# POOL's transfers by index without waits between them, and the heads' fetches moved from SyncE's queue to ACT's

## The chip, the cores and the metric

One core of one Trainium2 chip runs the kernel as one program. The metric is device time in microseconds (us). The engines are PE (TensorE, matrix products), DVE (VectorE), ACT (ScalarE), POOL (GpSimd) and SP (SyncE, which here only issues DMA transfers). Each engine works through its own list of instructions in order; a semaphore wait in that list holds up everything behind it on that engine and nothing on the others.

## The reference

A "macaron" block on x of 16 sequences x 512 tokens x 256 features, in float32: a mixture-of-experts feed-forward, attention, and the same feed-forward again.

```python
x = x + 0.5 * ffn(layernorm(x))
x = x + attention(layernorm(x))          # 16 heads of 16, ALiBi bias, 8 heads causal and 8 anti-causal
x = x + 0.5 * ffn(layernorm(x))

# ffn: 2 shared experts (256 -> 128 -> 256) for every token, and 16 routed ones (256 -> 64 -> 256)
out = einsum('tnm,nmd->td', silu(gs) * us, wd_s)
weights, indices = top_k(softmax(flat @ router_w), 2)
out += einsum('tem,emd->td', silu(g) * u * comb, wd_r)   # only the 2 chosen experts of a token count

# attention
out = softmax(q k^T / 4 + bias) v ; return out @ Wf + bf
```

## The kernel before

The unit of work is a sequence b (512 tokens, NT = 4 tiles of 128 partitions). Layer l = 0 is the first feed-forward, l = 1 the second. The sequences of a layer are worked in groups: (0 to 5), (6 to 15) in layer 0, and (0 to 6), (7 to 12), (13 to 15) in layer 1.

Routing. For each sequence DVE finds the two experts of each token and `position`, the row that the token gets in a DRAM tensor `sorted_x` in which the tokens of an expert lie together. POOL then **scatters** the normalised tokens `xn` there: 8 indirect transfers for each sequence and layer (2 choices x 4 tiles), each of 128 rows of 1 KB. When the whole group is in, tiles of 256 sorted rows are fetched by SP's queue (`t_x`, with the expert's weights `t_w`), PE multiplies, and the results go to `sorted_y`. For each sequence POOL then **fetches** its rows back (`y_tok<-sorted_y`, again 8 indirect transfers), and DVE's `combine` (L1646) adds them, weighted, to `x_att` (l = 0) or `x_ffn` (l = 1). There is one buffer `y_tok`, so the 8 fetches of the next sequence start behind the `combine` of this one; only the last group has four more, in `q_stack` and `k_stack`.

Waits of POOL. The scatters of a sequence count on 2 or 3 semaphores in turn (`sent[i][n % d]`), the fetches likewise (`gathered[i][n % d]`), where `apart_out` and `apart_back` give d: 3 for scatters of layer 0's first group and for fetches of layer 1 from sequence 6 on, else 2. Transfer n waits until transfer n - d has landed, so at most d of a sequence are under way:

```python
if n >= apart_out(l, b):
    pool.wait_ge(*sent[buffer][n % apart_out(l, b)].at(l, b, n - apart_out(l, b)))
```

Other work stands between these transfers in POOL's list: the causal masks of the attention weights (L1797 on `p_buf`, which PE's value products L1202 need), the low halves of the shared experts' hidden values (L1770 on `hs_buf`, which PE's down products L991 to L993 need), `qk_part` (L1784), `rstd` (L1726), and `o_pack` times the reciprocal `den` (L1803).

Heads. Attention handles 4 heads (a g of 4) at a time. PE leaves 4 heads' outputs and softmax denominators in a PSUM bank, ACT copies it to `o_raw` (L1350) and issues its transfer to DRAM, `o_store` (L1353). When g = 2m and 2m + 1 are there, the piece `heads` (b, m) fetches them back rearranged: `o_pack` (256 KB) and `den` (256 KB, each denominator row repeated for the 16 rows of its head). DVE takes the reciprocal of `den` in four parts (L1676), POOL multiplies, and PE projects (L1215) once both m are done. Before the change SP issues these two transfers (L925, L928), behind waits for both `o_store` transfers, for the projection of sequence b - 1, and for the last use of `den`.

The shift. For each g, ACT also sends 8 KB of row maxima into `q_stack` (L1367), and PE's score products of that g (L1182) wait for it.

Order. A planner (`Plan.run`) simulates the five engines with a cost and a due time for each piece and writes each engine's list; the engines then follow the lists, whatever the real times are. A piece `part(at, engine, cost, piece, needs..., takes..., lag)` is due at `at`, takes `cost`, and its result counts as there after `lag`. The planner knows the limit of d too (`some`), with a landing 2.2 us after the issue.

Of the kernel before, what the change touches and what calls it, by code (L numbers as in the profile page):

```python
# [15 lines left out]
B, S, D = 16, 512, 256  # L16
# [118 lines left out]
def y_buffer(l, b):  # L135
    return (b - Y_EARLY) % 5 if l == 1 and b >= Y_EARLY else 0

# [134 lines left out]
def schedule():  # L272
# [186 lines left out]
    for b in range(B):  # L459
# [32 lines left out]
        for m in range(2):  # L492
            heads = "heads", b, m
            at = t + 8 * m + 4 + 9.6
            part(at, "SP", 1.0, heads, (("o put", b, 2 * m), "ACT"), (("o put", b, 2 * m + 1), "ACT"),
                 takes=[(f"o_pack{m}", ("o_pack", b, m), [(("project", b, 1), "PE")]),
                        ("den", ("den", b, m), [(heads, "POOL")])], lag=4.0)
            for i in range(NT):
                part(at + 0.5 + 0.2 * i, "DVE", 0.85, ("heads", b, m, i), (heads, "SP"))
# [55 lines left out]
def build(nc, book, plan, a, out):  # L555
    ctx = ExitStack()
    with ctx:
# [147 lines left out]

        sent = [[signal(f"sent{i}{n}", 16) for n in range(3)] for i in range(6)]
        filled, filled_act = signal("filled", 16), signal("filled_act", 16)
        gathered = [[signal(f"gathered{i}{n}", 16) for n in range(3)] for i in range(5)]

        def all_sent(l, b):  # L710

            i, d = norm_buffer("ffn", l, b), apart_out(l, b)
            return [sent[i][n % d].at(l, b, n) for n in range(2 * NT - d, 2 * NT)]

        def all_gathered(l, b):
            i, d = y_buffer(l, b), apart_back(l, b)
            return [gathered[i][n % d].at(l, b, n) for n in range(2 * NT - d, 2 * NT)]
# [95 lines left out]
        def _(sp):  # L813
# [16 lines left out]
            def do(name, *of):  # L830
# [19 lines left out]
                elif name == "stack rows":  # L850

                    for b in EARLY:
                        sp.wait_ge(*x_put[0, b].at(b))
                        for landed in all_sent(0, b):
                            sp.wait_ge(*landed)
# [11 lines left out]
                elif name == "tile x":  # L867
                    l, g, j = of
                    i = x_home(l, g, j)
                    if j == 0:  # L870
# [7 lines left out]
                        for b in sent_all(l, g):  # L878
                            for landed in all_sent(l, b):
                                sp.wait_ge(*landed)  # L880
# [37 lines left out]
                elif name == "heads":  # L918
                    b, m = of
                    for i in range(2):  # L920
                        sp.wait_ge(*o_put[i].at(b, 2 * m + i))
                    if b:
                        sp.wait_ge(*proj_full.at(b - 1, 1))
                    heads = o_store[b, 2 * m:2 * m + 2].rearrange("g (h r) s -> (g h) r s", r=VR)
                    sp.dma_start(o_pack[:, m, :], heads[:, 0:HD, :]).then_inc(*o_got[m].step(b, 0))  # L925
                    if before["den", b, m]:
                        sp.wait_ge(*o_ready.at(*before["den", b, m][1:]))
# [297 lines left out]
        def _(act):  # L1225
            def do(name, *of):
# [37 lines left out]
                elif name == "norm":  # L1264
# [3 lines left out]
                    if before["xn", kind, l, b]:  # L1268
# [3 lines left out]
                        if old_kind == "ffn":  # L1272

                            for landed in all_sent(old_l, old):
                                act.wait_ge(*landed)
# [593 lines left out]
```

## Time and profile before

| what | us |
|---|---|
| median of 3 runs | 2264.89 |
| lowest and highest | 2262.14, 2269.9 |
| the profiled execution's own time | 2255.13 |
| its span, first to last instruction | 2253.3 |
| PE busy | 1702.2 (76%) |
| DVE busy | 1474.2 (65%) |
| ACT busy | 1046.5 (46%) |
| POOL busy | 947.3 (42%) |

Busy time counts neither waits nor the issuing of transfers by SP and ACT. A POOL indirect transfer counts as busy while POOL writes its descriptors (about 1 us). "POOL y_tok L1763 <- DMA" in a view of waits is idle time of POOL ahead of line 1763 that the landing of a transfer ended. The chain that ended last is followed back from the last instruction, at each step to what released it.

### The profile page before, as it was taken

The numbers are of one execution on the slowest core, as the hardware profiler recorded it, in microseconds if no ns is written. First come the engines' busy times: TensorE is split into PE (matmuls) and PEld (weight loads), VectorE is DVE, ScalarE is ACT, GpSimd is POOL, SyncE is SP. The second block draws the span as 40 slices with busy tenths as digits, with TensorE's granted clock in tenths as the row PEclk, the third lists the DMA queues.
The fourth block names the chain that finished last, engine by engine and source line by source line (L and its number), as shares of the span: only waits on it lengthen the run. The fifth ranks groups of instructions, "written<-read, shape, count | busy, mean of one in ns | idle before, by whom it ended". The sixth has DMA issues, their size and how long they took to land.

```text
span 2253.3 us, 35352 instructions
## 1 busy us (share of the span) xinstructions
PE 1702.2 (76%) x10696; PEld 1121.1 (50%) x10696; DVE 1474.2 (65%) x3920; ACT 1046.5 (46%) x2263; POOL 947.3 (42%) x999
## 2 busy tenths in 40 slices
PE   3758875678788888886877889888887677985382
PEld 2646655446455555543544546555554334553251
DVE  4765666677766657676677776766787757573432
ACT  3325543354455555554454555645554335553151
POOL 2643337454423231445444343443545635234604
PEclk8979996789999999988998989999998789997686
DMA  7468753645867666555449765666746686864895
GB/s 206 139 205 248 251 182 97 121 90 154 227 180 211 187 193 172 151 96 124 92 75 239 182 171 146 178 167 138 176 105 132 207 247 164 244 188 149 265 310 162
DMA packets 327979, 392.80 MB, mean 174 GB/s; under 512 B 40296, under 2 KB 269032, under 8 KB 327784
## 3 DMA queue, kind: packets, MB, share of 16 engines
q1 hardware_dynamic: 269520, 284.59, 48.4%
q0 software_dynamic: 24576, 67.14, 10.5%
q10 hardware_dynamic: 33696, 38.81, 5.2%
q8 instruction: 88, 1.44, 0.3%
q14 instruction: 99, 0.81, 0.1%
HBM read 188.58 MB, written 155.19 MB: 153 GB/s over the span
## 4 chain that ended last, share of the span: by engine, by line
PE 29%; DMA 26%; DVE 17%; issue 10%; POOL 10%; SPq 4%; ACT 3%; another core or an unknown queue 0%; ACTq 0%; DVEq 0%; POOLq 0%
DMA sorted_x<-xn,position 7%; DMA y_tok<-sorted_y,position 6%; DMA den<-o_store 4%; PE bank L1202 3%; PE bank L1098 3%; PE bank L991 3%; PE bank L1109 3%; PE bank L993 3%; PE bank L992 3%; PE bank L1182 2%; POOL sorted_x L1737 2%; DMA q_stack<-shift_t 2%; DVE x_att L1646 2%; PE bank L1215 2%; POOL y_tok L1763 2%
## 5 line engine op out<-in xcount | busy, mean ns | idle before, releaser
L1343 ACT ACTIVATE p_buf<-bank 128x512 f32<-128x512 f32 x640 | 361.8, 599 | 264.4 <-PE bank L1182 212.1
L1574 DVE TENSOR_REDUCE row_max<-bank 128x1 f32<-128x512 f32 (+2 forms) x768 | 349.2, 504 | 76.4 <-PE bank L1165 70.6
L1737 POOL DMA_INDIRECT sorted_x<-xn,position x224 | 221.4, 988 | 232.6 <-DMA sorted_x<-xn,position 140.4
L1797 POOL TENSOR_SCALAR_AFFINE_SELECT p_buf<-p_buf 128x512 f32<-128x512 f32 x256 | 161.6, 645 | 316.5 <-ACT p_buf L1343 314.9
L1182 PE MATMUL bank<-q_stack,k_stack 101*128 101x512 bf16 (+3 forms) x1024 | 244.7, 318 | 57.2 <-DMA q_stack<-shift_t 46.6
L1149 PE MATMUL bank<-k_stack,q_stack 99*128 99x512 bf16 (+3 forms) x1024 | 254.2, 319 | 32.4 <-issue 19.6
L1763 POOL DMA_INDIRECT y_tok<-sorted_y,position x192 | 185.5, 966 | 213.2 <-DMA y_tok<-sorted_y,position 117.0
L1202 PE MATMUL bank<-p_buf,v_rows 128*32 128x512 f32 (+3 forms) x2048 | 197.5, 485 | 91.0 <-POOL p_buf L1797 88.0
L1309 ACT ACTIVATE t_y<-bank 128x256 f32<-128x256 f32 x406 | 133.3, 380 | 156.4 <-PE bank L1109 137.4
L991 PE MATMUL bank<-w_down,hs_buf 128*128 128x256 f32 x256 | 89.1, 348 | 126.5 <-POOL hs_buf L1770 125.4
L1676 DVE RECIPROCAL den<-den 128x128 f32<-128x128 f32 x128 | 110.0, 913 | 101.2 <-DMA den<-o_store 99.8
L1098 PE MATMUL bank<-t_xt,t_w 128*128 128x256 f32 x548 | 156.8, 413 | 21.2 <-DMA t_w<-expert_w 12.1
L1165 PE MATMUL bank<-cbf 128*128 128x256 bf16 (+1 forms) x640 | 169.7, 265 | 0.0
L1182 PEld LDWEIGHTS bank<-q_stack,k_stack 101*128 101x128 bf16 x1024 | 85.4, 101 | 162.3 <-issue 61.8
L1627 DVE SCALAR_TENSOR_TENSOR t_g<-t_th,bank 64x256 f32<-64x256 f32 x203 | 82.5, 406 | 119.3 <-ACT t_th L1300 110.2
L1149 PEld LDWEIGHTS bank<-k_stack,q_stack 99*128 99x128 bf16 x1024 | 94.2, 102 | 127.3 <-issue 67.1
L1294 ACT ACTIVATE t_xt<-bank 128x512 f32<-128x512 f32 x203 | 118.7, 596 | 64.3 <-PE bank L1088 50.6
L1300 ACT ACTIVATE t_th<-bank 64x256 f32<-64x256 f32 x203 | 76.3, 376 | 147.3 <-PE bank L1098 105.7
L1202 PEld LDWEIGHTS bank<-p_buf,v_rows 128*32 128x32 f32 x2048 | 50.0, 115 | 171.2 <-POOL p_buf L1797 112.4
L991 PEld LDWEIGHTS bank<-w_down,hs_buf 128*128 128x128 f32 x256 | 60.4, 236 | 140.5 <-issue 139.7
L1098 PEld LDWEIGHTS bank<-t_xt,t_w 128*128 128x128 f32 x548 | 102.0, 202 | 53.6 <-issue 24.3
L1632 DVE TENSOR_TENSOR t_h<-bank,t_g 64x128 f32<-64x128 f32 x406 | 119.2, 293 | 13.3
(193 smaller groups left out, 3910.7 us busy)
## 6 DMA issues: line engine op xcount, KB each, us to landing
t_w<-expert_w SPq DMA_DIRECT2D x137, 256.0 KB
t_x<-sorted_x SPq DMA_DIRECT2D x137, 256.0 KB
sorted_y<-t_y SPq DMA_DIRECT2D x137, 256.0 KB
q_stack<-qk_part SPq DMA_DIRECT2D x192, 128.0 KB
k_stack<-qk_part SPq DMA_DIRECT2D x192, 128.0 KB
sorted_x<-zeros SPq DMA_DIRECT2D x69, 256.0 KB, 3.6
p_buf<-expert_w SPq DMA_DIRECT2D x66, 256.0 KB
p_buf<-sorted_x SPq DMA_DIRECT2D x66, 256.0 KB
```

Source lines behind the costliest of these rows:

```text
L991: pe.matmul(dst, left(0), right(0), start=first, stop=False, skip_group_check=True)
L1098: ins = pe.matmul(ps[:, 0:RT], weights[:, P * d:P * d + P], xt[:, d, :], start=(d == 0), stop=(d == ND - 1))
L1149: pe.matmul(ps[:, col:col + k1 - k0], q_stack[0:ROWS_S, h, P * qt:P * qt + P], k_stack[0:ROWS_S, h, k0:k1], start=(n == 0), stop=False, sk ...
L1165: ins = pe.matmul(dst, ident_bf, mask, start=False, stop=True, skip_group_check=True)
L1182: ins = pe.matmul(ps[:, col:col + q1 - q0], k_stack[0:ROWS_P, h, P * kt:P * kt + P], q_stack[0:ROWS_P, h, q0:q1], start=(n == 0), stop=Tru ...
L1202: ins = pe.matmul(ps[VR * hh:VR * hh + VR, q0:q1], v_rows[b % 2][:, v0:v0 + VR], p_of(u)[:, col:col + q1 - q0], start=(r == 0), stop=(r == 2),
L1309: act.activation(t_y[i][:, t, :], psum("ty", *of, t)[:, 0:D], ACT.Copy).then_inc(*ty_out.step(*of, t))
L1343: act.activation(p_of(u), psum("score", *of)[:, :], ACT.Exp).then_inc(*exp_done.step(*of))
L1574: ins = dve.tensor_reduce(row_max[g % 2][:, n:n + 1], src[:, col:col + q1 - q0], X, ALU.max)
L1737: pool.indirect_dma_start(sorted_x[l, group_of(l, b)], bass.IndirectOffsetOnAxis(ap=position[:, b, k, t:t + 1], axis=0), xn[buffer][:, t, ...
L1763: pool.indirect_dma_start(y[:, k, t, :], None, sorted_y[l, g], bass.IndirectOffsetOnAxis(ap=position[:, b, k, t:t + 1], axis=0)).then_inc( ...
L1797: pool.affine_select(blocks, blocks, [[0, GH], [1 if ahead else -1, P]], ALU.is_ge, zero, base=0, channel_multiplier=-1 if ahead else 1).t ...
```

## The change

Two things. (1) POOL issues the 8 scatters and the 8 fetches of a sequence without waiting for landings between them; one semaphore for each buffer counts all 8, and whoever needs them waits for the full count. (2) The piece `heads` goes from SP's list to ACT's, with a planned cost of 1.2 instead of 1.0 us. The planner still plans with the limit d, but since the piece is on another engine, it writes other lists for all engines from sequence 0's first `heads` on.

```diff
@@ planner @@
-            part(at, "SP", 1.0, heads, (("o put", b, 2 * m), "ACT"), (("o put", b, 2 * m + 1), "ACT"),
+            part(at, "ACT", 1.2, heads, (("o put", b, 2 * m), "ACT"), (("o put", b, 2 * m + 1), "ACT"),
...
-                part(at + 0.5 + 0.2 * i, "DVE", 0.85, ("heads", b, m, i), (heads, "SP"))
+                part(at + 0.5 + 0.2 * i, "DVE", 0.85, ("heads", b, m, i), (heads, "ACT"))
@@ semaphores @@
-        sent = [[signal(f"sent{i}{n}", 16) for n in range(3)] for i in range(6)]
+        sent = [signal(f"sent{i}", 16) for i in range(6)]
-        gathered = [[signal(f"gathered{i}{n}", 16) for n in range(3)] for i in range(5)]
+        gathered = [signal(f"gathered{i}", 16) for i in range(5)]
...
-            i, d = norm_buffer("ffn", l, b), apart_out(l, b)
-            return [sent[i][n % d].at(l, b, n) for n in range(2 * NT - d, 2 * NT)]
+            return sent[norm_buffer("ffn", l, b)].at(l, b, 2 * NT - 1)
@@ SP, and now ACT @@
-                elif name == "heads":
-                    ... sp.wait_ge, sp.dma_start ...
+                elif name == "heads":
+                    b, m = of
+                    for i in range(2):
+                        act.wait_ge(*o_put[i].at(b, 2 * m + i))
+                    if b:
+                        act.wait_ge(*proj_full.at(b - 1, 1))
+                    heads = o_store[b, 2 * m:2 * m + 2].rearrange("g (h r) s -> (g h) r s", r=VR)
+                    act.dma_start(o_pack[:, m, :], heads[:, 0:HD, :]).then_inc(*o_got[m].step(b, 0))
+                    if before["den", b, m]:
+                        act.wait_ge(*o_ready.at(*before["den", b, m][1:]))
+                    act.dma_start(den[:, :], heads[:, HD:VW, :].broadcast_to((HB, HD, S))).then_inc(*o_got[m].step(b, 1))
@@ POOL, scatter @@
-                    if n >= apart_out(l, b):
-                        pool.wait_ge(*sent[buffer][n % apart_out(l, b)].at(l, b, n - apart_out(l, b)))
...
-                        xn[buffer][:, t, :], None).then_inc(*sent[buffer][n % apart_out(l, b)].step(*of))
+                        xn[buffer][:, t, :], None).then_inc(*sent[buffer].step(*of))
@@ POOL, fetch @@
-                    y, landed = tail_y[y_buffer(l, b)], gathered[y_buffer(l, b)][n % apart_back(l, b)]
-                    if n >= apart_back(l, b):
-                        pool.wait_ge(*landed.at(l, b, n - apart_back(l, b)))
+                    y, landed = tail_y[y_buffer(l, b)], gathered[y_buffer(l, b)]
```

POOL's list before at the scatters of layer 1, sequence 3 (927 us in the profile); `sent00` and `sent01` are the two landing counts.

```order
L1770 TENSOR_TENSOR hs_buf<-h_buf,hs_buf 128x512 [waits h_hi]
L1797 AFFINE_SELECT p_buf<-p_buf 128x4x128 [waits exp_done]
L1737 DMA sorted_x<-xn,position 86272x256 [waits place_step]
L1737 DMA sorted_x<-xn,position 86272x256
L1737 DMA sorted_x<-xn,position 86272x256 [waits sent00]
L1737 DMA sorted_x<-xn,position 86272x256 [waits sent01]
L1737 DMA sorted_x<-xn,position 86272x256 [waits sent00]
L1737 DMA sorted_x<-xn,position 86272x256 [waits sent01]
L1770 TENSOR_TENSOR hs_buf<-h_buf,hs_buf 128x512 [waits h_hi]
L1737 DMA sorted_x<-xn,position 86272x256 [waits sent00]
L1737 DMA sorted_x<-xn,position 86272x256 [waits sent01]
L1797 AFFINE_SELECT p_buf<-p_buf 128x4x128 [waits exp_done]
```

POOL's list now at the same scatters.

```order
L1755 TENSOR_TENSOR hs_buf<-h_buf,hs_buf 128x512 [waits h_hi]
L1725 DMA sorted_x<-xn,position 86272x256 [waits place_step]
L1725 DMA sorted_x<-xn,position 86272x256
L1782 AFFINE_SELECT p_buf<-p_buf 128x4x128 [waits exp_done]
L1755 TENSOR_TENSOR hs_buf<-h_buf,hs_buf 128x512 [waits h_hi]
L1725 DMA sorted_x<-xn,position 86272x256 x2
L1769 TENSOR_TENSOR qk_part<-rest,qk_part 128x512 [waits qk_second]
L1725 DMA sorted_x<-xn,position 86272x256 x2
L1782 AFFINE_SELECT p_buf<-p_buf 128x4x128 [waits exp_done]
L1782 AFFINE_SELECT p_buf<-p_buf 128x4x128
L1725 DMA sorted_x<-xn,position 86272x256 x2
L1788 TENSOR_TENSOR o_pack<-o_pack,den 128x512 [waits den_done,o_got0]
```

Only the first scatter still waits for something (the positions). A `qk_part` and two more masks now also stand among the scatters, and `o_pack` follows them at once.

SP's list before at `heads` (1, 1), 634 us in the profile.

```order
L939 DMA k_stack<-qk_part 16x8x512 [waits qk_third,score_full]
L939 DMA k_stack<-qk_part 16x8x512 x5
L901 DMA sorted_y<-t_y 128x2x256 [waits ty_out]
L925 DMA o_pack<-o_store 128x1x512 [waits proj_full,o_put1,o_put0]
L928 DMA den<-o_store 128x1x512 [waits o_ready]
L883 TENSOR_LOAD tile_i [waits tx_full]
L884 ISA
L884 DMA t_x<-sorted_x 128x2x256
```

ACT's list before from `o_raw` of sequence 1, g = 3 on (625 us in the profile).

```order
L1350 ACTIVATE o_raw<-bank 128x512 [waits o_put0,o_full]
L1353 DMA o_store<-o_raw 128x512 [waits o_copied]
L1309 ACTIVATE t_y<-bank 128x256 [waits ty_put_sp1,ty_full]
L1309 ACTIVATE t_y<-bank 128x256
L1294 ACTIVATE t_xt<-bank 128x512 [waits tgu_full,tx_full]
L1343 ACTIVATE p_buf<-bank 128x512 [waits score_full] x2
L1239 ACTIVATE act_t<-bank 128x512 [waits qk_full,v_full,xt_full]
L1343 ACTIVATE p_buf<-bank 128x512 [waits score_full]
L1239 ACTIVATE act_t<-bank 128x512 [waits xt_full]
L1300 ACTIVATE t_th<-bank 64x256 [waits th_step,tgu_full]
L1343 ACTIVATE p_buf<-bank 128x512 [waits o_full,score_full]
L1343 ACTIVATE p_buf<-bank 128x512 [waits score_full]
```

ACT's list now, from the same `o_raw` on.

```order
L1332 ACTIVATE o_raw<-bank 128x512 [waits o_put0,o_full]
L1335 DMA o_store<-o_raw 128x512 [waits o_copied]
L1291 ACTIVATE t_y<-bank 128x256 [waits ty_put_sp2,ty_full]
L1291 ACTIVATE t_y<-bank 128x256
L1325 ACTIVATE p_buf<-bank 128x512 [waits score_full]
L1276 ACTIVATE t_xt<-bank 128x512 [waits tgu_full,tx_full]
L1325 ACTIVATE p_buf<-bank 128x512 [waits score_full]
L1222 ACTIVATE act_t<-bank 128x512 [waits qk_full,v_full,xt_full]
L1282 ACTIVATE t_th<-bank 64x256 [waits th_step,tgu_full]
L1358 DMA o_pack<-o_store 128x1x512 [waits proj_full,o_put1,o_put0]
L1361 DMA den<-o_store 128x1x512 [waits o_ready]
L1282 ACTIVATE t_th<-bank 64x256 [waits th_step,tgu_full]
```

The two transfers stand seven pieces behind the `o_store` transfer (counting the two rows of `t_y` as one), and wait there for its landing and for the projection; they no longer stand behind SP's transfers into `k_stack`. Tile work and scores follow them in ACT's list.

## Rows read from the trace of the kernel before

**Rows 1.** The page, head and part 1: busy us (share) and instructions.
```profile
span 2253.3 us, 35352 instructions
...
PE 1702.2 (76%) x10696; PEld 1121.1 (50%) x10696; DVE 1474.2 (65%) x3920; ACT 1046.5 (46%) x2263; POOL 947.3 (42%) x999
```

**Rows 2.** The chain that ended last, whole span: shares by line; then start, us, what.
```profile
by line: issue 10.4%; DMA sorted_x<-xn,position 6.8%; DMA y_tok<-sorted_y,position 6.3%; DMA den<-o_store 3.5%; PE bank L1202 3.5%; PE bank L1098 3.5%; PE bank L991 3.0%; PE bank L1109 2.8%; PE bank L993 2.7%; PE bank L992 2.6%; PE bank L11
...
634.58 9.19 DMA den<-o_store
...
1637.37 4.59 DMA den<-o_store
```

**Rows 3.** Waits, whole span: us in total, times, longest us.
```profile
POOL sorted_x L1737 <- DMA sorted_x<-xn,position: 140.4, 80, 5.2
...
POOL y_tok L1763 <- DMA y_tok<-sorted_y,position: 117.0, 62, 5.6
...
DVE den L1676 <- DMA den<-o_store: 99.8, 23, 11.7
...
PE bank L1182 <- DMA q_stack<-shift_t: 46.6, 19, 7.6
```

**Rows 4.** Timeline of POOL, 925 to 947 us: start, us, idle before.
```profile
931.96 0.96 POOL L1737 DMA_INDIRECT sorted_x<-xn,position  x1 [2.62 <-DMA sorted_x<-xn,position]
...
938.43 0.96 POOL L1737 DMA_INDIRECT sorted_x<-xn,position  x1 [4.25 <-DMA sorted_x<-xn,position]
...
940.85 1.27 POOL L1770 TENSOR_TENSOR hs_buf<-h_buf,hs_buf 128x512 fp32r<-128x512 f32 x1
```

**Rows 5.** Timeline of PE, 934 to 944 us.
```profile
942.38 0.55 PE L991 MATMUL bank<-w_down,hs_buf 128*128 128x256 f32 x1 [6.05 <-POOL hs_buf L1770]
```

**Rows 6.** Timeline of POOL in the first group, 60 to 112 us.
```profile
81.89 1.03 POOL L1737 DMA_INDIRECT sorted_x<-k_stack,position  x1 [0.18 <-issue]
...
92.05 0.98 POOL L1737 DMA_INDIRECT sorted_x<-k_stack,position  x1 [0.30 <-issue]
```

**Rows 7.** Line 1763, all transfers whose landing is known.
```profile
DMA to landing us min/median/max: 2.7/2.9/4.1
```

**Rows 8.** Windows: us, busy us of each engine, clock, DMA share, GB/s.
```profile
165.00:420.00 255.00, 194.12 (x1057) 144.40 (x1056) 153.65 (x472) 109.03 (x257) 115.65 (x111) 0.88 0.65 192
420.00:1715.00 1295.00, 1064.90 (x7081) 675.70 (x7079) 916.99 (x2305) 675.63 (x1425) 532.88 (x574) 0.92 0.63 155
1715.00:1880.00 165.00, 113.15 (x664) 65.64 (x665) 110.48 (x274) 60.56 (x124) 84.19 (x93) 0.82 0.72 201
2000.00:2253.00 253.00, 134.22 (x745) 90.45 (x743) 108.26 (x307) 80.00 (x197) 102.16 (x106) 0.76 0.68 220
```

**Rows 9.** Waits of PE, 420 to 1715 us.
```profile
PE bank L1202 <- POOL p_buf L1797: 64.7, 40, 6.7
PE bank L991 <- POOL hs_buf L1770: 41.1, 10, 6.8
```

**Rows 10.** Waits of PE, 165 to 420 us.
```profile
PE bank L991 <- POOL hs_buf L1770: 24.7, 5, 15.3
```

**Rows 11.** Waits, 1715 to 1880 us.
```profile
POOL y_tok L1763 <- DMA y_tok<-sorted_y,position: 33.3, 17, 4.7
```

**Rows 12.** Waits of POOL, 2000 to 2253 us.
```profile
POOL sorted_x L1737 <- DMA sorted_x<-xn,position: 11.8, 8, 2.7
```

**Rows 13.** The chain, 600 to 650 us: start, us, what.
```profile
625.27 0.33 ACTq L1353
...
633.85 0.68 SPq L925
```

**Rows 14.** The page, part 3: DMA queues (q1 SP's, q0 POOL's, q10 ACT's).
```profile
q1 hardware_dynamic: 269520, 284.59, 48.4%
q0 software_dynamic: 24576, 67.14, 10.5%
q10 hardware_dynamic: 33696, 38.81, 5.2%
```

## What the change should do, before it was run

> **What bounds the kernel now.** I read the page first. PE is busy for 76% of the span, ACT for 46%, POOL for 42% [rows 1], so no engine is full and the time is set by how they wait for each other. The chain that ended last says where: the landings of indexed transfers are 6.8% + 6.3% of 2253.3 us, 153 + 142 = 295 us, and those of `den` 3.5%, 79 us [rows 2]. The reader is to see that no line of PE has more than 3.5%. The waits say who stood: POOL sat idle 140.4 us for landings of scatters and 117.0 us for landings of fetches, 257 us in 142 waits, 1.8 us each; DVE 99.8 us for `den` [rows 3].
>
> An idle POOL costs nothing by itself, so next comes what stood behind it in its list. In the timeline at 926 us POOL waited 2.62 and 4.25 us for scatters that nobody else needed yet, then ran the `hs_buf` subtraction at 940.85 [rows 4], and PE, idle for 6.05 us, started its down product behind that at 942.38 [rows 5]. 6.87 us of POOL's waiting thus became 6.05 us of PE's. Between 420 and 1715 us PE waited 64.7 us for masks and 41.1 us for `hs_buf`, both POOL's work [rows 9]; between 165 and 420 us it was 24.7 us [rows 10]. The windows give the room: PE idle for 61 of 255, 230 of 1295, 52 of 165 and 119 of 253 us [rows 8].
>
> **The change: waits of POOL.** What is left of a transfer is its issue, 0.96 to 1.0 us, and 0.30 us between two. The first group shows eight scatters and one subtraction going out with hardly a wait: from 81.89 to 92.05 us seven intervals, less 1.3 us for the subtraction, make (10.16 - 1.3) / 7 = 1.27 us each [rows 6]. Eight take 10.2 us. I take the gain stage by stage, each between nothing (all hidden behind another chain) and POOL's whole idle time.
> - 165 to 420 us: at most the 24.7 us of [rows 10]. The same stretch also waits for inputs to be loaded and stored; I take half, 12 us.
> - 420 to 1715 us: PE waited 64.7 + 41.1 = 105.8 us for POOL [rows 9]. A mask may be late because ACT's exponentials were, which the change leaves as they are; I take half, 53 us, between 0 and 105.8.
> - 1715 to 1880 us: fetches into the one `y_tok`, DVE's sum, the next fetches. Everything is in series, and POOL's landing waits of 33.3 us [rows 11] lie on it. The last landing of eight will come somewhat later than now against its issue; I take 28 us.
> - 2000 to 2253 us: POOL waited 11.8 us for scatters [rows 12] and a little for fetches, with the transfer engines at 68% and 220 GB/s [rows 8], the highest rate of the four; 8 us.
>
> Together 101 us; bounds 0 and 257.
>
> How fast a landing is decides this. Where a landing of a fetch is known by itself it took 2.7 to 4.1 us, 2.9 in the middle [rows 7]; in the loaded stretch a pair held POOL for 4.25 us more after 0.30 us and an issue of 0.96 us each [rows 4]. The Trainium skill, "DMA: Bandwidth & Descriptors", section on the anatomy of one DMA on the gpsimd path, fits 2.0 us plus bytes over 436e3 to a transfer: 2.3 us for these 128 KB. By that estimate POOL would stand 1.0 us instead of 0.30 behind a pair, three times in each of 64 sets of eight: 134 us in all, and the term would be half of mine, about 50 us. The trace has 257 us of idle time, and I go by it.
>
> **The change: heads on ACT.** Removed from SP: 32 times two issues. At 625.27 us ACT sent off `o_store`; SP issued `o_pack` at 633.85 for 0.68 us [rows 13], behind stack transfers in its list, and `den`, issued at 634.58, took 9.19 us to land; another one took 4.59 [rows 2]. SP's queue carried 284.59 MB and was busy 48.4% of the span, ACT's 38.81 MB and 5.2% [rows 14], so on ACT's queue `den` has less ahead of it. 79 us on the chain at 9.19 us are about 9 landings. Halfway to 4.59 us saves 2.3 us each, 21 us (bounds 0 and 41).
>
> Added to ACT: two issues of about 0.68 us [rows 13], 1.4 us, 32 times, 44 us. ACT is busy 46% [rows 1]; scores for PE stand behind them, and a quarter on the path makes 10 us (bounds 0 and 44). ACT also waits there for the landing of `o_store`. Six pieces lie between, and SP, whose list has the same wait, was through it 8.6 us after `o_store` was sent off [rows 13]; I cost this wait at nothing, covered by those six pieces. Without them ACT would stand for up to 8.6 us each time. Last, the 8 KB shift of the next g follows 512 KB of heads on ACT's queue. PE already waits 46.6 us for shifts, 19 times of 64 [rows 3]. If half of the 19 come 1 us later, that is 10 us (bounds 0 and 64).
>
> **Contention.** No byte is added, but bursts are denser: up to eight of POOL's transfers under way for two or three now. 67.14 MB in 24576 packets is 2.7 KB a packet, SP's 1.06 KB [rows 14], so where both queues are full POOL's takes the larger share. Others then wait: 5 us, between 0 and the rival's price below. The other lists of the planner I cost at nothing either way: same pieces, other neighbours; random shifts of some us.
>
> **Sum.** 2255 (the profiled execution's own time) - 101 - 21 + 10 + 10 + 5 = 2158. The median of the runs shown is 2264.9, 9.8 us above that execution, so I add 10 for the usual run: 2168 us, 4.3% faster. Its own range is 2080 to 2235.
>
> **Rivals.**
> 1. Another chain is as long. POOL comes free, but PE at 82% in the long stretch (1065 of 1295 us, [rows 8]), DVE and the loads take over after a third of the gain: 34 us, about 2232. For it: only PE's 6.05 us of idle time, in one place, is shown to follow from POOL's waits. Against it: PE has 230 us idle there.
> 2. All of POOL's idle time comes back, with a shorter chain for everyone: 2265 - 257 = 2008. It needs every wait on the path; most of the 142 waits aren't.
> 3. The waits move into the issue: with more than three or four transfers under way the descriptor queue is full and POOL stands in its issue instead. Then only a few us change, 2265. For it: the trace never has eight of a sequence in flight under load. Against it: the issues of [rows 6] take 1.0 us each for a whole sequence and more.
> 4. Slower: POOL's bursts and the heads push back the 8 KB shifts and `den`. Each of 64 shifts has PE's scores of four heads behind it. At 2 us more each that is 128 us, less the 101 + 21 above: about 2271, and from 1.9 us a shift on the change loses. For it: packets of POOL's queue are 2.6 times as large as SP's [rows 14]. The Trainium skill, "DMA: Bandwidth & Descriptors", section on queues, rings and completion order, says that each DMA engine takes turns between its queues packet by packet, which by itself speaks for a larger share of large packets. Against it: the shift is a transfer of ACT's queue and gets its turn early, and the transfer engines were busy only 63% [rows 8].
>
> **Chances.** Forecast (2% to 8% faster) 0.60; rival 1 (0.3% to 2%) 0.14; rival 2 0.04; rival 3 0.07; rival 4 0.15. A measurement here can tell about 0.3% from no change. Faster 0.60 + 0.14 + 0.04 = 0.78, same 0.07, slower 0.15. The range of 8 in 10 reaches from 2080 to 2266: rival 1 and half of rival 3 are inside, rival 2 and rival 4 out.
>
> **What would show it.** POOL's idle time for landings ahead of its scatters and fetches is gone, and issues follow each other at 1.27 us with no issue above 1.7 us (rival 3: issues of several us). PE's waits for masks and `hs_buf` fall from 105.8 to about 50 us in the long stretch; the windows of the single `y_tok` shorten by 4 us a sequence. `den` lands in 6 to 7 us, and DVE's wait for it falls below 80 us. PE's wait for shifts stays under 60 us; above 100 us rival 4 holds. ACT's wait for `o_store` is under 20 us in all. The prediction is wrong if PE's idle time is merely booked to other releasers, or if ACT stands in `heads` for landings or for the projection of sequence b - 1, which I couldn't price from a row.

## The result

The changed kernel takes 2194.3 us (median of 4 runs, 2189.3 to 2198.2) against 2263.5 us before (4 runs). The ratio is 0.969 [0.966, 0.9721]: 3.1% faster. The forecast was 2168 us, 4.3% faster, with a range of 2080 to 2266 us.

The page of the changed kernel, head and parts 1 and 3 (queues: packets, MB, share):

```profile
span 2196.4 us, 35275 instructions
...
PE 1697.9 (77%) x10696; PEld 1117.4 (51%) x10696; DVE 1469.6 (67%) x3920; ACT 1043.5 (48%) x2263; POOL 949.1 (43%) x999
...
q1 hardware_dynamic: 260816, 267.81, 47.0%
q0 software_dynamic: 24576, 67.14, 10.9%
q10 hardware_dynamic: 42400, 55.59, 8.1%
```

Against [rows 1] no engine has less to do; the span is 57 us shorter and the shares went up by one or two points. Against [rows 14] the heads' 16.8 MB went from q1 to q10.

Its waits over the whole span (us in total, times, longest us; L1725 is the scatter, L1748 the fetch, L1667 the reciprocal, L1165 the score product, L974 the down product):

```profile
DVE den L1667 <- DMA den<-o_store: 102.0, 26, 11.8
...
POOL sorted_x L1725 <- issue: 61.4, 225, 0.5
...
PE bank L1165 <- DMA q_stack<-shift_t: 45.3, 16, 5.3
...
POOL y_tok L1748 <- issue: 42.1, 152, 2.2
...
PE bank L974 <- POOL hs_buf L1755: 38.6, 8, 15.0
```

Of [rows 3] both POOL rows are gone: no transfer by index waits for a landing any more, only for the 0.3 us of issue between two. DVE's wait for `den` did not fall (99.8, now 102.0 us), and PE's for the shift neither rose nor fell by much (46.6, now 45.3). The value product's group on the page shows PE's idle time for masks:

```profile
L1185 PE MATMUL bank<-p_buf,v_rows 128*32 128x512 f32 (+3 forms) x2048 | 188.8, 467 | 26.6 <-POOL p_buf L1782 19.2
```

That is 19.2 us where it was 88.0; PE's wait for `hs_buf` went from 125.4 to 38.6. But one wait of the same kind, the longest, has only changed its name in the view. Before, in layer 1's last sequence, it is put down to POOL:

```profile
2124.98 0.55 PE L991 MATMUL bank<-w_down,hs_buf 128*128 128x256 f32 x1 [29.80 <-POOL hs_buf L1770]
```

In the changed kernel the profile names no releaser, yet POOL's subtraction ends at 2067.43 us and PE starts at 2067.69:

```profile
2066.15 1.28 POOL L1755 TENSOR_TENSOR hs_buf<-h_buf,hs_buf 128x512 fp32r<-128x512 f32 x1
2067.69 0.55 PE L974 MATMUL bank<-w_down,hs_buf 128*128 128x256 f32 x1 [26.13 <-issue]
```

Counted with POOL's, PE's waits for masks and `hs_buf` go from 213.4 to 84 us. PE thus waits some 130 us less for POOL, and the span is 57 us shorter. Where the other 73 us went is the question of this study.

The same place as in [rows 4] and [rows 5], scatters of layer 1, sequence 3, in POOL's timeline now (start, us, idle before):

```profile
903.22 0.96 POOL L1725 DMA_INDIRECT sorted_x<-xn,position  x1 [0.30 <-issue]
904.49 0.96 POOL L1725 DMA_INDIRECT sorted_x<-xn,position  x1 [0.30 <-issue]
905.76 0.96 POOL L1725 DMA_INDIRECT sorted_x<-xn,position  x1 [0.31 <-issue]
907.03 0.96 POOL L1725 DMA_INDIRECT sorted_x<-xn,position  x1 [0.30 <-issue]
910.74 1.27 POOL L1755 TENSOR_TENSOR hs_buf<-h_buf,hs_buf 128x512 fp32r<-128x512 f32 x1 [2.75 <-ACT hs_buf L1246]
```

The first six scatters start at 900.59 us, 901.96 and from there on every 1.27 us, and at the second `hs_buf` subtraction POOL now waits for ACT (2.75 us), where before ACT had been ready and POOL stood for landings. The work behind the transfers is as early as ACT lets it be. By the two timelines POOL's list is the same at this place before and after: six scatters, the subtraction, two scatters, a mask. The list that is given above under "POOL's list now at the same scatters" is the one at the scatters of sequence 4 (987 us in the changed kernel), so that the `qk_part` and the masks between the scatters are no news of sequence 3.

**Where the time came from.** The lists are marked by the start of the reciprocals of sequence 0's first heads, of sequence 12's second, and of sequence 14's first. Before, these marks lie at 481, 1713 and 1895 us (windows: us, busy us of PE, PEld, DVE, ACT, POOL, clock, DMA share, GB/s):

```profile
0.00:481.00 481.00, 330.58 (x1849) 248.03 (x1850) 299.81 (x935) 193.93 (x426) 222.06 (x220) 0.87 0.61 177
481.00:1713.00 1232.00, 1018.81 (x6781) 648.68 (x6780) 875.13 (x2203) 642.86 (x1362) 499.18 (x540) 0.93 0.63 158
1713.00:1895.00 182.00, 127.57 (x757) 74.83 (x753) 124.81 (x316) 72.14 (x148) 97.75 (x105) 0.84 0.70 196
1895.00:2253.00 358.00, 225.22 (x1313) 149.58 (x1313) 174.48 (x467) 137.57 (x330) 128.33 (x135) 0.81 0.72 216
```

In the changed kernel they lie at 466, 1681 and 1847 us:

```profile
0.00:466.00 466.00, 329.84 (x1832) 250.74 (x1832) 303.95 (x936) 192.14 (x424) 221.13 (x219) 0.87 0.62 183
466.00:1681.00 1215.00, 1017.36 (x6792) 641.47 (x6792) 867.86 (x2200) 642.37 (x1363) 506.42 (x546) 0.93 0.65 160
1681.00:1847.00 166.00, 129.05 (x790) 77.34 (x790) 125.46 (x334) 74.45 (x158) 93.75 (x100) 0.87 0.79 222
1847.00:2196.00 349.00, 221.68 (x1287) 147.81 (x1285) 172.32 (x453) 134.55 (x319) 127.80 (x134) 0.81 0.71 217
```

The reader is to see four differences: -15 us up to the first mark, -17 us in the long stretch, -16 us in the 182 us after it, -9 us at the end. In the long stretch PE's idle time went from 1232 - 1019 = 213 to 1215 - 1017 = 198 us. Its waits for POOL there had been, before,

```profile
PE bank L1202 <- POOL p_buf L1797: 61.1, 37, 6.7
...
PE bank L991 <- POOL hs_buf L1770: 35.1, 9, 6.8
```

96.2 us, and in the changed kernel (L1185 the value product, L974 the down product) they are

```profile
PE bank L1132 <- issue: 31.9, 10, 10.1
PE bank L1165 <- DMA q_stack<-shift_t: 31.1, 12, 5.0
PE bank L1092 <- DVE t_h L1624: 18.2, 11, 6.3
PE bank L1185 <- POOL p_buf L1782: 13.0, 20, 1.7
PE bank L1071 <- DMA t_x<-sorted_x: 10.5, 4, 7.7
...
PE bank L1154 <- DVE shift L1660: 9.8, 8, 2.0
...
PE bank L974 <- POOL hs_buf L1755: 3.8, 3, 1.8
```

13.0 + 3.8 = 16.8 us (L1185 and L974). So 79 us of waits for POOL went away and 15 us of idle time went with them; the rest came back ahead of the row products (L1132, 31.9 us for which the profile shows no releaser, 11.6 before), the tiles that SP loads (L1071, 10.5 for 3.8) and the shift's transpose (L1154, 9.8 for 4.0), and in many smaller pieces. With all rows of the view added up by who came last, PE's waits in this stretch went from 97 to 20 us for POOL, from 46 to 64 for DVE, from 4 to 18 for ACT, and from 16 to 43 where the profile shows no releaser.

### The profile page after: what moved, and what is told of

It reads as the page before. It is cut to its first block and busy times, and to the rows that moved or that the text cites. A ratio compares the mean times of both kernels' runs of the same rounds, so it can differ in the third digit from the quotient of the medians.

```text
span 2196.4 us, 35275 instructions
## 1 busy us (share of the span) xinstructions
PE 1697.9 (77%) x10696; PEld 1117.4 (51%) x10696; DVE 1469.6 (67%) x3920; ACT 1043.5 (48%) x2263; POOL 949.1 (43%) x999
## 5 line engine op out<-in xcount | busy, mean ns | idle before, releaser
L1132 PE MATMUL bank<-k_stack,q_stack 99*128 99x512 bf16 (+3 forms) x1024 | 254.3, 320 | 64.6 <-issue 44.3
L1165 PE MATMUL bank<-q_stack,k_stack 101*128 101x512 bf16 (+3 forms) x1024 | 244.6, 321 | 67.5 <-DMA q_stack<-shift_t 45.3
L1725 POOL DMA_INDIRECT sorted_x<-xn,position x224 | 221.8, 990 | 101.5 <-issue 52.9
L1748 POOL DMA_INDIRECT y_tok<-sorted_y,position x192 | 186.1, 969 | 118.9 <-issue 42.1
L1185 PE MATMUL bank<-p_buf,v_rows 128*32 128x512 f32 (+3 forms) x2048 | 188.8, 467 | 26.6 <-POOL p_buf L1782 19.2
L1667 DVE RECIPROCAL den<-den 128x128 f32<-128x128 f32 x128 | 110.2, 915 | 102.1 <-DMA den<-o_store 102.0
L1132 PEld LDWEIGHTS bank<-k_stack,q_stack 99*128 99x128 bf16 x1024 | 92.8, 102 | 166.2 <-issue 101.8
L1165 PEld LDWEIGHTS bank<-q_stack,k_stack 101*128 101x128 bf16 x1024 | 87.6, 102 | 164.7 <-issue 57.5
L974 PE MATMUL bank<-w_down,hs_buf 128*128 128x256 f32 x256 | 88.5, 346 | 68.8 <-POOL hs_buf L1755 38.6
L1092 PE MATMUL bank<-t_w,t_h 64*128 64x256 f32 x548 | 102.8, 453 | 32.6 <-DVE t_h L1624 27.3
L1755 POOL TENSOR_TENSOR hs_buf<-h_buf,hs_buf 128x512 fp32r<-128x512 f32 x64 | 81.7, 1277 | 100.4 <-ACT hs_buf L1246 98.1
```

Of the source, the lines that this page charges most:

```text
L1132: pe.matmul(ps[:, col:col + k1 - k0], q_stack[0:ROWS_S, h, P * qt:P * qt + P], k_stack[0:ROWS_S, h, k0:k1], start=(n == 0), stop=False, sk ...
L1165: ins = pe.matmul(ps[:, col:col + q1 - q0], k_stack[0:ROWS_P, h, P * kt:P * kt + P], q_stack[0:ROWS_P, h, q0:q1], start=(n == 0), stop=Tru ...
L1185: ins = pe.matmul(ps[VR * hh:VR * hh + VR, q0:q1], v_rows[b % 2][:, v0:v0 + VR], p_of(u)[:, col:col + q1 - q0], start=(r == 0), stop=(r == 2),
L1725: pool.indirect_dma_start(sorted_x[l, group_of(l, b)], bass.IndirectOffsetOnAxis(ap=position[:, b, k, t:t + 1], axis=0), xn[buffer][:, t, ...
L1748: pool.indirect_dma_start(y[:, k, t, :], None, sorted_y[l, g], bass.IndirectOffsetOnAxis(ap=position[:, b, k, t:t + 1], axis=0)).then_inc( ...
```

## The experiments

All ratios are to the kernel before, with a 95% interval. The ratio of the plain medians can differ from them by up to 0.4%, and it is given where that matters. The lists of the engines are those of before where it says so.

**The waits alone.** The changed kernel with the heads put back to SP; all lists as before.

```diff
-            part(at, "ACT", 1.2, heads, (("o put", b, 2 * m), "ACT"), ...
+            part(at, "SP", 1.0, heads, (("o put", b, 2 * m), "ACT"), ...
-                elif name == "heads":      # in ACT's program
+                elif name == "heads":      # in SP's program
```

> The kernel before with the landing waits of POOL removed and the heads left on SyncE's list; every engine's list is the same as before. Theory W (the waits are the whole gain, the heads give nothing, since DVE's wait for den went from 99.8 to 102.0 us): 0.969 of before, about 2194 us. Theory H (the heads' move brings a third or more): 0.978 to 0.985, 2213 to 2229 us. Theory O (the planner's other lists hide a loss or bring a gain of the size of 1%): 0.959 or 0.979. Under W and O the waits of PE for masks and hs_buf fall from 213 us (88.0 + 125.4) to about 60 us as in the changed kernel.

Measured: 0.9665 [0.9637, 0.9694], 2192.9 us; the median of the kernel before is 2262.3 us in the same series, which by itself gives 0.9693. Theory W holds: the waits are the whole gain, and theory H is out. PE's waits for masks and `hs_buf` fell to 26.2 + 65.0 = 91 us. The 60 us of the expectation had been read off the changed kernel without its wait of 26.13 us; with it, 91 stands against 84. The marks came at 461, 1686 and 1852 us, the end at 2198: -20, -7, -16 and -12 us. With the lists untouched, the long stretch gained 7 us: PE's idle time there fell by 23 us, from 213 to 190, but its busy time was 16 us longer. What came in the place of POOL is DVE. Ahead of the routed experts' second product PE waited in that stretch, before,

```profile
PE bank L1109 <- DVE t_h L1632: 18.3, 10, 5.1
```

and in this kernel

```profile
PE bank L1103 <- DVE t_h L1624: 33.8, 16, 5.1
```

All rows added up, PE's waits went from 97 to 23 us for POOL and from 46 to 79 us for DVE.

**The heads alone.** The kernel before with only the piece `heads` moved to ACT, lists as in the changed kernel.

```diff
-            part(at, "SP", 1.0, heads, (("o put", b, 2 * m), "ACT"), ...
+            part(at, "ACT", 1.2, heads, (("o put", b, 2 * m), "ACT"), ...
```

> The kernel before with only the heads moved to ACT (planned cost 1.2 us, lists as in the changed kernel), POOL's landing waits kept. Theory W: no difference, 0.997 to 1.003. Theory H: 0.98 to 0.99. Theory O: anything between 0.99 and 1.01, and then the run with only the planned cost changed moves as far. The sum that was made ahead (21 us gained at den, 20 us lost at ACT and the shifts) says 0.9995.

Measured: 1.0006 [0.9978, 1.0035]. No difference, as theory W and the sum had it.

**One under way.** Each transfer waits for the one ahead; lists as before.

```diff
+def real_out(l, b):
+    return 1
+def real_back(l, b):
+    return 1
-                    if n >= apart_out(l, b):
+                    if n >= real_out(l, b):
...
```

> The kernel before with each of POOL's scatters and fetches waiting for the landing of the one just ahead of it (one under way instead of two or three); lists unchanged. If POOL's idle time reaches the end time at the rate that the change showed (69 us of 257 us idle), and one transfer alone takes 3 to 4 us from issue to landing, 448 waits of some 2 to 3 us each give 900 to 1300 us of idle time in place of 257, and the time rises by 170 to 280 us, to 1.08 to 1.12. If the first microseconds of a wait are hidden and only the long ones count, the rise is larger than that rate says: above 1.15. If the gain of the change had another source than the waits, it stays below 1.03.

Measured: 1.2653 [1.2613, 1.2693], 2867.7 us, far above the rise that the rate of the change would give. POOL's waits for landings in this kernel (us, times, longest):

```profile
POOL sorted_x L1745 <- DMA sorted_x<-xn,position: 418.2, 182, 7.8
...
POOL y_tok L1771 <- DMA y_tok<-sorted_y,position: 395.3, 145, 8.0
...
POOL q_stack L1771 <- DMA q_stack<-sorted_y,position: 65.3, 28, 4.5
...
POOL k_stack L1771 <- DMA k_stack<-sorted_y,position: 65.1, 27, 4.3
...
POOL sorted_x L1745 <- DMA sorted_x<-k_stack,position: 59.2, 28, 4.0
```

They add up to 1003 us, as expected. It is their price that was not: 600 us for 736 us more of idle time, 0.81 us for each. From before to no waits at all it is 0.0335 x 2262 = 76 us for 267 us, 0.28 for each. PE waited 364.4 + 300.9 = 665 us for `hs_buf` and masks, against 213 us before: here POOL is what everything waits for. Of the 600 us some 77 are PE's own: it was busy 1779 us for 1702, at a granted clock of 0.80 for 0.89.

**Three under way everywhere.** The same edit with 3 in place of 1.

> The kernel before with three transfers of a sequence under way everywhere (before: two in most stretches, three in some); lists unchanged. From one under way (1.265, 1003 us of POOL idle for landings) to before (267 us) each us of idle time cost 0.81 us; from before to none it cost 0.28 us. If this flattening goes on, three under way leave some 100 us of idle time, and these last ones cost next to nothing: 0.970. If idle time costs 0.28 us each all the way down: 0.979. If the third transfer under way brings nothing, because landings are limited by bandwidth: above 0.99.

Measured: 0.9714 [0.9673, 0.9756]. Its two largest waits of POOL for landings:

```profile
POOL y_tok L1771 <- DMA y_tok<-sorted_y,position: 44.2, 24, 4.0
...
POOL sorted_x L1745 <- DMA sorted_x<-xn,position: 39.1, 31, 2.7
```

With three small ones they make 90 us. Going from 267 to 90 us of idle time brought 2.9%, 65 us; the last 90 us brought some 11 us more, and by the intervals that may be nothing. The idle time left with three under way is nearly free.

**Scatters only.** Scatters without waits, fetches with theirs; lists as before.

```diff
-                    if n >= apart_out(l, b):
-                        pool.wait_ge(*sent[buffer][n % apart_out(l, b)].at(l, b, n - apart_out(l, b)))
```

> The kernel before without the landing waits between scatters; fetches keep theirs; lists unchanged. Scatters hold 141 of the 267 us of POOL's idle time for landings. If idle time counts alike wherever it is, this brings 53% of what the waits alone brought (0.9665): 0.982. If the fetches are worth more, since DVE's sums and the next sequence wait for them in series: 0.988. If scatters are worth more, since PE waited for hs_buf behind them (125 us): 0.976.

Measured: 0.9831 [0.9799, 0.9864]: half of the gain of the waits for half of their idle time (1.7% of 3.35%). Scatters and fetches count alike, as far as this run tells: the fetches' half is what is left over, and the fetches alone were not tried.

**The planner freed of the limit.** The changed kernel, and the waits alone, with lists planned for transfers that follow each other at once.

```diff
-            some = [(("scatter", l, b, n - d), "POOL landed")] if n >= d else []
+            some = []
-            some = [(("fetch", l, b, n - d), "POOL landed")] if n >= d else []
+            some = []
```

> The changed kernel (no landing waits, heads on ACT) with the planner freed of the limit too, so that the lists are written for transfers that follow each other at once. If the lists were what held back the gain in the long stretch, the time falls to 0.95 to 0.96. If not, it is one more set of lists and lies within 0.5% of the changed kernel: 0.964 to 0.974.

> The same with the heads on SyncE: 0.95 to 0.96 if the lists held back the gain, else within 0.5% of the run with the waits alone, 0.9665.

Measured: heads on ACT 1.0011 [0.9987, 1.0036], heads on SP 0.9955 [0.9936, 0.9974]. Neither expectation held: with these lists the whole gain, or 29 of 34 thousandths of it, is lost. The timeline of POOL in the kernel with the heads on SP, behind sequence 12:

```profile
1713.87 1.04 POOL L1748 DMA_INDIRECT y_tok<-sorted_y,position  x1 [2.62 <-DVE x_ffn L1637]
...
1722.73 0.95 POOL L1748 DMA_INDIRECT y_tok<-sorted_y,position  x1 [0.30 <-issue]
...
1726.96 0.63 POOL L1782 TENSOR_SCALAR_AFFINE_SELECT p_buf<-p_buf 128x512 f32<-128x512 f32 x1
...
1785.23 0.98 POOL L1748 DMA_INDIRECT y_tok<-sorted_y,position  x1 [16.18 <-DVE x_ffn L1637]
```

Eight fetches now stand as one block of 10 us (1713.87 to 1723.7) with a mask only at 1726.96, and further on POOL stands 16.18 us for DVE's sum of the sequence before. In the lists that are planned with the limit, masks, `qk_part` and `hs_buf` stand between the transfers, mostly behind every second one. From the reciprocals of sequence 12's second heads to those of sequence 13's first this kernel takes 103 us (1703 to 1806), the kernel with the waits alone 42 us (1686 to 1728). That is 61 us, more than the whole difference of 51 us between their spans. Which part of it is due to the blocks of eight and which to the order of DVE's sums was not tried apart.

**One number of the planner.** The kernel before with the heads' planned cost at 1.2 us, and the same without the waits.

```diff
-            part(at, "SP", 1.0, heads, (("o put", b, 2 * m), "ACT"), ...
+            part(at, "SP", 1.2, heads, (("o put", b, 2 * m), "ACT"), ...
```

> The kernel before with one number of the planner changed: the planned cost of the heads on SyncE is 1.2 and not 1.0 us. It does the same work with the same waits, but 1260 of PE's 2658 places and as large a share of the other lists are written differently. Theory O: up to 1% off, 0.99 or 1.01. Theories W and H: within 0.3%.

> The kernel with the waits alone removed, with the lists of the run with the planned cost 1.2 (0.996 with the waits). If what the waits bring doesn't depend on the lists: 0.996 x 0.9665 = 0.963. If it does, as with the freed planner, anything from 0.955 to 0.98.

Measured: 0.9961 [0.9925, 0.9996] with the waits, 0.9707 [0.9662, 0.9753] without. By these ratios the waits bring 2.5% on these lists, 3.35% on the lists of before, and 0.969 / 1.0006, 3.2%, on those of the changed kernel. The product of the expectation, 0.963, lies just outside the interval. But its first factor has an interval of its own, and the plain medians show no difference: 2187.7 against 2257.8 us is 3.1% on these lists, 2192.9 against 2262.3 us is 3.1% on those of before. So it is not shown that the gain of the waits depends on these lists.

**The heads moved by hand.** The waits alone removed, and the 32 heads taken from SP's list and put seven places behind `o put` in ACT's; every other place as before.

```diff
     plan.run()
+    for b in range(B):
+        for m in range(2):
+            heads, put = ("heads", b, m), ("o put", b, 2 * m + 1)
+            plan.order["SP"].remove(heads)
+            at = plan.order["ACT"].index(put)
+            plan.order["ACT"].insert(at + (1 if (b, m) == (B - 1, 1) else 7), heads)
```

> The kernel with the waits alone removed and every list as before, except that the 32 heads are taken out of SyncE's list and put into ACT's, seven places behind the second o_store transfer of each pair (the last one directly behind it). It tells the move of the heads from the new lists that came with it. If the move as such is worth nothing: 0.964 to 0.969. If it gains (den lands sooner) and the new lists lost that again: 0.955 to 0.961. If it costs and the lists made up for it: above 0.971.

Measured: 0.9731 [0.9683, 0.978], against 0.9665 [0.9637, 0.9694] with the heads on SP. The intervals just touch; the medians, 2196.1 and 2192.9 us, are 0.15% apart. The move as such brings nothing. Whether it costs some tenths of a per cent these runs cannot tell.

**What holds the long stretch now.** On the kernel with the waits alone, masks cut from 128 to 8 columns, and reciprocals cut from 128 to 8.

```diff
-                    act.activation(p_of(u), psum("score", *of)[:, :], ACT.Exp)...
+                    act.activation(p_of(u), psum("score", *of)[:, :], ACT.Exp, scale=0.01)...
-                        blocks = whole[:, :, col:col + P]
+                        blocks = whole[:, :, col:col + 8]
...
```

> The kernel with the waits alone removed (0.9665), with POOL's causal masks cut from 128 to 8 columns of each block, so that most of the masking is left out (and the exponentials taken of a hundredth of the scores, at the same cost). POOL has some 100 us less to do, and each mask is there about 0.5 us sooner. If POOL is no longer what the end waits for, little happens: at most the 26 us that PE still waits for masks, 0.955 to 0.967. If POOL still sets the pace, 0.93 to 0.95.

```diff
-                    part = den[:, P * i:P * i + P]
+                    part = den[:, P * i:P * i + 8]
```

> The kernel with the waits alone removed, with the reciprocals of den cut from 128 to 8 columns of each part, so that most denominators are not inverted. DVE has some 100 us less to do and the way from den's landing to the projection is some 3 us shorter, 32 times. If DVE and the heads' way are what holds the long stretch now that POOL doesn't: 0.935 to 0.955. If PE itself with its list in order is the bound: above 0.96.

Measured: masks 0.9682 [0.9636, 0.9727], reciprocals 0.9491 [0.944, 0.9541]. The long stretch, in the window between the same marks, of the kernel with the waits alone,

```profile
461.00:1686.00 1225.00, 1034.65 (x6772) 657.16 (x6771) 870.76 (x2203) 644.52 (x1362) 506.66 (x545) 0.91 0.63 159
```

of the one with small masks,

```profile
463.00:1677.00 1214.00, 1027.88 (x6796) 653.39 (x6789) 851.29 (x2204) 644.45 (x1364) 424.31 (x545) 0.92 0.63 160
```

and of the one with small reciprocals (columns as above: PE, PEld, DVE, ACT, POOL):

```profile
465.00:1630.00 1165.00, 1015.19 (x6800) 647.35 (x6792) 799.67 (x2205) 644.34 (x1364) 507.18 (x546) 0.94 0.67 167
```

Taking 82 us of POOL's work from the stretch shortened it by 11 us in one profile, and the whole kernel by nothing that can be measured (DVE was busy 19 us less there too; why is not known). Taking 71 us of DVE's shortened it by 60 us, 20 of them PE's own busy time (1035 and 1015 us, at a granted clock of 0.91 and 0.94); the medians of the whole kernel are 54 us apart. With the waits gone the masks are off the path of the long stretch; DVE, or the way from `den` through DVE to the projection, is on it. Whether it is DVE's time or the length of that way this run does not tell: it shortens both. It says nothing of the end, where PE still stands some 25 us in all three kernels for POOL's last subtraction, behind transfers that no longer wait for each other.

## Why the prediction was right, and where its sizes were off

**Right.** The direction, the source (POOL's waits), the range, and 2% to 8% as the likeliest case. Issues of POOL follow each other at 1.27 us, and the longest takes as long as before (1.66 us), so rival 3, a full descriptor queue, did not happen. PE's wait for shifts stayed where it was, so rival 4 did not either. The wait of ACT that is put down to the landing of `o_store` in the changed kernel:

```profile
L1335 ACTq DMA_DIRECT2D o_store<-o_raw x64: 320/322/399, 436.8 to 2001.4; - x64
...
  ACT p_buf L1325: 8.9, 2
  ACT t_y L1291: 2.3, 1
```

11.2 us in all, under the 20 us that was forecast. That is not all that ACT stands there. Its timeline also shows it idle directly ahead of `o_pack`'s issues, up to 3.4 us at a time and 31 us ahead of the 32 together, and the profile books that time, with the two issues, to no releaser:

```profile
1637.66 0.65 ACTq L1358 DMA_DIRECT2D o_pack<-o_store  x1
...
1639.03 1.57 ACT L1325 ACTIVATE p_buf<-bank 128x512 f32<-128x512 f32 x3 [4.80 <-issue]
```

So whether ACT's wait stayed under 20 us is open, and the wait that was costed at nothing is not nothing; the run with the heads alone shows that it did not reach the end time. Of the two signs of being wrong that the prediction named, the first, PE's idle time booked to other releasers, largely came true in the long stretch: 79 us less waiting for POOL, 15 us less idle time.

**The term of the waits, 101 us, was too large.** Measured it is 76 us by the ratio of the run with the waits alone, 69 us by the medians. By stages the forecast had 12, 53, 28 and 8 us; the run has 20, 7, 16 and 12 at its marks, and the changed kernel 15, 17, 16 and 9 (the marks bound the stages nearly, not exactly, as the forecast's windows do). The step that failed is "PE waited 105.8 us for POOL; I take half, 53 us". PE's wait for POOL fell by 79 us in that stretch, more than the 56 us forecast, and still gave 7 to 17 us. A row "PE waited for POOL" says who came last, not how much later than the next. The next were nearly as late: with the same lists PE's waits for DVE rose from 46 to 79 us as those for POOL went, and the run with small reciprocals shortened the stretch by up to 60 us. Rival 1, another chain as long, thus held in the long stretch, and the forecast in the others. That the total came as near as it did is in part luck: the long stretch gave 36 to 46 us less than its term, the first and the last stage together up to 12 us more.

The single place that was shown for it, 6.87 us of POOL's idle time and 6.05 us of PE's, was a true one and no fair sample. Up to the first mark the opposite error was made: the wait of 24.7 us was halved too, and the stretch gave 15 to 20 us.

**The fetches into one `y_tok`,** 28 us forecast, gave 16. The 33.3 us of waits for landings went, but the fetches have masks between them in POOL's list, and POOL's waits for ACT's exponentials ahead of those masks grew from 3.3 to 17.8 us in this stretch. A wait in the same list took the place of 14.5 of the 33.3 us, and another 7.8 us, none before, went to the reciprocals ahead of `o_pack` (in the run with the waits alone the two are 10.1 and 9.3 us). POOL's wait for DVE's sums stayed (25.1, now 23.7 us).

**The lower estimate of the same term.** The Trainium skill, "DMA: Bandwidth & Descriptors", section on the anatomy of one DMA on the gpsimd path, has the fit that gives 2.3 us for 128 KB, and by that estimate the term came to about 50 us; by the idle time it came to 101, and the measured 69 to 76 us lie between. The trace does not agree with the 2.3 us for these transfers by index: where their landing is known they took 2.7 to 4.1 us [rows 7]. The idle time itself was 267 us (with the last group's and the first's few, beyond the 257 of [rows 3]), twice the 134 us that the estimate gave.

**The heads: the sum 21 - 10 - 10 was right at its total and in none of its parts, which is luck.** "On ACT's queue `den` has less ahead of it" failed. From issue to the first reciprocal, where DVE waited for the landing, it took 7.3 us on average on SP's queue (23 cases of before) and 8.4 us on ACT's (26 of the changed kernel), worked out from the timelines; on equal lists without waits it is 7.7 us on SP's (heads left there) and 7.8 on ACT's (heads moved by hand), and over all 32 first reciprocals 7.5 and 8.2 us. The costs did not reach the end time either: with the heads alone moved the ratio is 1.0006, and the shifts were not later. Planner and contention were costed at about nothing: contention may be so, the planner's lists need not be. One planned cost moved by 0.2 us changed the time by 0.4%, hardly clear of the noise (0.2% by the medians), but lists that were planned without the limit lost nearly the whole gain of the waits. The changed kernel's lists are still planned with pauses between the transfers that no longer exist, and the one other kind of list that was tried, without these pauses, is the slower one.

**What stays open.** How 79 us less waiting for POOL turned into 15 us less idle time of PE is settled as to place and as to what PE waits for instead (DVE, ACT, and 43 us with no releaser shown), but not wait by wait. The granted clock of the long stretch was 0.91 in the profile of the waits alone, 0.93 before and in the changed kernel; PE was busy 1035 us there against 1019 and 1017. That is 16 us which would make the 7 us into more, and one profile of each cannot tell it from chance.

## What to carry to other kernels

The price of an engine's idle time is not a constant of the kernel. Here the same waits cost 0.8 us for each us of idle time while they were long, 0.28 on average over the last 267 us, and next to nothing in the last 90 (part of the first figure is a lower granted clock): a limit of three under way already had most of the gain. Before pricing a wait by who waits for it, ask how late the next one is, and test that by shrinking the next one's work.

A wait without a releaser in the view is not a wait for nothing. Look at what ended just before it before counting it out.

When engines follow lists that a planner wrote, a changed plan is an experiment of its own. Measure the change on the old lists first; the size of what new lists do (about 3% here) is that of the effect under study.

## What was not expected of the hardware

Eight transfers by index (128 rows of 1 KB each) issued without a wait cost POOL no more than two at a time: most took 0.96 to 1.0 us with 0.30 us between them, and the longest 1.66 us as before, in all stretches, also where the 16 transfer engines were busy 79% of the time (the window from 1681 to 1847 us). How many of them are under way at once was not measured. With a landing 2.7 to 4.1 us after the start where it is known [rows 7], some 6.5 us in the loaded stretch (from 931.96 to 938.43 us in [rows 4]), and 1.27 us from one to the next, an estimate is two to five, not eight. And a fetch of 256 KB of repeated rows landed no sooner on the queue that carried 55.6 MB (8.1%) than on the one that carried 267.8 MB or more (47%), so the backlog of its own issuer's queue did not show in it; what it does wait for was not found.
